# An attention pass in a graph kernel: weight and decay read from one PSUM bank, by two relus and two exponentials, in place of two banks and two exponentials

## The reference, cut to what matters

```python
f_src = (feat @ W_src.T + b_src)          # and f_dst, f_v likewise
a = f_src[src] + f_dst[dst]
e = jnp.where(a >= 0, a, 0.2 * a)         # the score of an edge
seg_max = segment_max(e, dst)
ex = jnp.exp(e - seg_max[dst])
sa = ex / segment_sum(ex, dst)[dst]
rst = segment_sum(f_v[src] * sa, dst)
```

## Time and profile before

| | |
|---|---|
| time, median of 3 runs | 4219.99 us (4213.49 to 4231.76) |
| the profiled execution | 4217.84 us, its span from first to last instruction 4216.0 us |
| busy over the span | PE 2904.7 us (69%), DVE 2103.0 us (50%), POOL 1590.1 us (38%), ACT 780.2 us (19%) |
| chain that ended last | PE 46%, DVE 18%, another core or an unknown queue 12%, DMA 11%, issue 7% |
| mean granted clock of PE | 0.780 of 2.4 GHz |

### The profile page before, as it was taken

How to read it: one execution, slowest core, us unless ns; L and a number is a source line. 1 busy time by engine, 2 the same in 40 slices (tenths; PEclk the granted TensorE clock), 3 DMA queues, 4 the chain that set the end, 5 groups by cost and what they waited for, 6 DMA issues and landing times.

```text
span 4216.0 us, 49450 instructions
## 1 busy us (share of the span) xinstructions
PE 2904.7 (69%) x14303; PEld 1742.8 (41%) x14451; DVE 2103.0 (50%) x4819; ACT 780.2 (19%) x1986; POOL 1590.1 (38%) x1665
## 2 busy tenths in 40 slices
PE   1444534444444666879677774999999999999188
PEld 1333323333333221434322222666666666666044
DVE  4555565555555322331300122777777777777420
ACT  0001101010100000100010011444444444444100
POOL 1656436666666100030000006555555556554200
PEclk6555555555555899889899956999999999999597
DMA  9940094000000899013179704778777878786142
GB/s 393 374 154 1 5 358 153 1 1 1 1 1 1 330 407 372 0 59 103 57 268 320 264 25 133 230 239 241 239 235 241 242 237 247 235 244 203 57 142 72
DMA packets 460279, 725.77 MB, mean 172 GB/s; under 512 B 64483, under 2 KB 334862, under 8 KB 460206
## 3 DMA queue, kind: packets, MB, share of 16 engines
q1 hardware_dynamic: 388154, 611.92, 41.6%
q0 software_dynamic: 65680, 109.05, 9.8%
q10 hardware_dynamic: 6372, 3.91, 0.3%
HBM read 443.75 MB, written 280.94 MB: 172 GB/s over the span
## 4 chain that ended last, share of the span: by engine, by line
PE 46%; DVE 18%; another core or an unknown queue 12%; DMA 11%; issue 7%; ACTq 2%; ACT 2%; POOL 1%; DVEq 1%; SPq 0%; POOLq 0%
DMA G<-adj_d 11%; PE PS L559 7%; DVE G L1225 6%; PE PS L738 5%; DVE G L1224 5%; PE PS L767 4%; PE PS L762 4%; PE PS L794 3%; PE PS L796 3%; PE PS L795 3%; PE PS L761 2%; PE PS L746 2%; PE PS L829 1%; PE PS L711 1%
## 5 line engine op out<-in xcount | busy, mean ns | idle before, releaser
L511 POOL DMA_INDIRECT adj_d<-D,place x782 | 748.8, 958 | 636.3 <-DVE place L1236 439.1
L498 POOL DMA_INDIRECT G<-tab_sv,src_e x784 | 748.7, 955 | 538.7 <-issue 288.4
L605 PE MATMUL PS<-wst,G 128*128 128x4 bf16 x1564 | 104.3, 171 | 637.2 <-DVE G L1225 600.2
L595 PE MATMUL PS<-ident,kst 128*128 128x128 f32 x1564 | 464.9, 453 | 86.8 <-ACT wst L1030 60.0
L595 PEld LDWEIGHTS PS<-ident,kst 128*128 128x128 f32 x1564 | 361.4, 321 | 92.8 <-ACT wst L1030 60.3
L1224 DVE SCALAR_TENSOR_TENSOR G<-PS,kst,tri 128x128 bf16<-128x128 f32 x782 | 271.0, 347 | 251.6 <-remote 146.9
L605 PEld LDWEIGHTS PS<-wst,G 128*128 128x128 bf16 x1564 | 72.3, 107 | 749.7 <-DVE G L1225 600.5
L1225 DVE TENSOR_SCALAR G<-PS,kst 128x256 bf16<-128x256 f32 x782 | 371.8, 475 | 0.0
L1440 DVE TENSOR_TENSOR_SCAN RB<-mring,RB,PS 128x512 f32<-128x512 bf16 x196 | 251.2, 1281 | 150.7 <-issue 78.9
L1029 ACT ACTIVATE kst<-G 128x2 f32 (+1 forms) x391 | 79.4, 203 | 1085.9 <-DVE place L1236 948.5
L528 POOL DMA_INDIRECT run_d<-V,head_i x25 | 24.0, 959 | 677.4 <-ACT V L1108 670.0
(11 more groups left out here) (324 smaller groups left out, 4871.9 us busy)
## 6 DMA issues: line engine op xcount, KB each, us to landing
G<-adj_d SPq DMA_DIRECT2D x350, 512.0 KB, 5.7
frac_d<-OSF SPq DMA_DIRECT2D x196, 512.0 KB
adj_d<-RB SPq DMA_DIRECT2D x7, 12800.0 KB, 54.5
run_d<-RB SPq DMA_DIRECT2D x4, 12992.0 KB
VT<-run_d SPq DMA_DIRECT2D x196, 256.0 KB
mring<-cut_d SPq DMA_DIRECT2D x196, 128.0 KB
HTx<-seg_d SPq DMA_DIRECT2D x196, 128.0 KB
OSF<-cnt_d SPq DMA_DIRECT2D x42, 512.0 KB
```

The source lines that it names most:

```text
L498: pool.indirect_dma_start(dest, None, table, bass.IndirectOffsetOnAxis(ap=idx, axis=0)).then_inc(done, 16)
L511: pool.indirect_dma_start(adj_d, bass.IndirectOffsetOnAxis(ap=place[:, w, k:k + 1], axis=0), pay[:, w, k, :], None).then_inc(sgr[g % 2], 16)
L595: last = nc.tensor.matmul(PS[:, r % 2, k * P:(k + 1) * P], kst[:, r, k:k + 1].to_broadcast([P, P]), ident[:, :], start=True, stop=True)
```

## The change

The new maximum is no longer needed for the exponentials. With d = e - (m + mring), weight = exp(-relu(-d)) and decay = exp(-relu(d)): where the score is above the old maximum, the weight is 1 and the decay exp(-d); elsewhere the decay is 1 and the weight exp(d). So PE adds only -RB(old) and -mring to bank q. ACT then reads bank q twice, relu(-d) to `D01` and relu(d) to bank 4+q, and takes the exponential of each in place. `gx` now comes after the relus, when bank q is free again; a new semaphore `gp`, after the exponentials, is what DVE's `weighted` waits for. The wait for `gback` (that `numerator` of chunk c-2 is done with bank 4+q and `D01`) goes from PE's difference matmuls; ACT has it before its first relu. `identb` becomes `nidentb`, the negative identity in bf16.

```diff
@@ PE, att_pass.body
                         if q == 0:
                             pe.wait_ge(carried, i * (R // 2) + h // 2 + 1)
-                        if not (first and h < 2):
-                            pe.wait_ge(gback, GB * (c - 2) + GB)
-                        nc.tensor.matmul(PS[:, 4 + q, :], ident[:, :], RB[:, q * CE:(q + 1) * CE], start=True, stop=False)
-                        nc.tensor.matmul(PS[:, 4 + q, :], nident[:, :], RB[:, q * CE + 1:(q + 1) * CE + 1], start=False, stop=False)
-                        nc.tensor.matmul(PS[:, q, :], nident[:, :], RB[:, q * CE + 1:(q + 1) * CE + 1], start=False, stop=True, skip_group_check=True)
-                        nc.tensor.matmul(PS[:, 4 + q, :], identb[:, :], mring[:, h, :], start=False, stop=True).then_inc(dif, 1)
+                        nc.tensor.matmul(PS[:, q, :], nident[:, :], RB[:, q * CE:(q + 1) * CE], start=False, stop=False, skip_group_check=True)
+                        nc.tensor.matmul(PS[:, q, :], nidentb[:, :], mring[:, h, :], start=False, stop=True, skip_group_check=True).then_inc(dif, 1)
@@ ACT, att_pass.body
                         act.wait_ge(dif, c + 1)
-                        nc.scalar.activation(PS[:, 4 + q, :], PS[:, 4 + q, :], ACT.Exp)
                         if not (first and h < 2):
                             act.wait_ge(gback, GB * (c - 2) + GB)
-                        nc.scalar.activation(D01[:, q, CE:2 * CE], PS[:, q, :], ACT.Exp).then_inc(gx, 1)
+                        nc.scalar.activation(D01[:, q, CE:2 * CE], PS[:, q, :], ACT.Relu, scale=-1.0)
+                        nc.scalar.activation(PS[:, 4 + q, :], PS[:, q, :], ACT.Relu).then_inc(gx, 1)
+                        act.wait_ge(gx, c + 1)
+                        nc.scalar.activation(D01[:, q, CE:2 * CE], D01[:, q, CE:2 * CE], ACT.Exp, scale=-1.0)
+                        nc.scalar.activation(PS[:, 4 + q, :], PS[:, 4 + q, :], ACT.Exp, scale=-1.0).then_inc(gp, 1)
@@ DVE, weighted
-                    dve.wait_ge(gx, c + 1)
+                    dve.wait_ge(gp, c + 1)
```

More of the change, by code:

```diff
@@ L119, in build @@
         onesb = sb("onesb", [P, TILE], bf16)
-        identb = sb("identb", [P, P], bf16)
+        nidentb = sb("nidentb", [P, P], bf16)
         nident = sb("nident", [P, P])
@@ L281, in build @@
         gx = sem("gx")
+        gp = sem("gp")
         gfront = sem("gfront")
@@ L1279, in _ @@
                 v.tensor_scalar(hdj[:, j, :], hd[:, :], float(-j * CW), None, ALU.add)
-            step(v.tensor_copy(identb[:, :], ident[:, :]))
+            step(v.tensor_copy(nidentb[:, :], nident[:, :]))
             dve.wait_ge(pst, 7)
```

## The result

| | before | after |
|---|---|---|
| median (range) | 4217.65 us (4213.49 to 4231.76) | 4363.16 us (4360.91 to 4378.95) |
| the profiled execution | 4217.84 us | 4378.95 us, span 4377.1 us |
| pace of the attention loop | 6.58 us a chunk | 7.43 us a chunk |

A forecast was written before the change was run, and what follows sets the result against it. PE at 6.30 us a chunk was taken to bound the kernel. Afterwards DMA's 5.25 + 0.28 + 0.07 of stalls make 5.60; 4217.84 - 195 x (6.58 - 5.60) = 4027, set to 4029 us for the median; range 3940 to 4135.

The forecast's parts named there:

- PE falls to 4.58 us a chunk: Attention loop: removing two f32 matmuls over 512 columns takes PE's work from 6.30 to 4.58 us a chunk.
- ACT's added 1.15 us: Attention loop: two more activations and ACT's own wait add 1.0 to 1.4 us a chunk, taken as 1.15.
- The longer chain closes at 4.85: Attention loop: the chain from maximum scan through relus and exponentials fits a 4.85 us pace, so added ACT work costs nothing.
- The DMA bound, 5.25 us: Attention loop: with PE shortened, DMA binds next, moving 1.57 MB a chunk at 299 GB/s in 5.25 us.
- The stalls, 0.35 us a chunk: Attention loop: unexplained ACT waits before `fifth` grow with ACT's list, from 0.28 to 0.35 us a chunk, added to the bound.
- the clock falls: Attention loop, chance 0.06: PE's gaps bring 1.2 GHz, 9.16 us for such a chunk; slower than before from x = 0.28.

The follow-up runs named there:

- e14: Changed kernel with POOL gathering source rows for the first four chunks only, on a slow-kind chip: 3851.35 us, ratio 0.9246.
- e8: Changed kernel with POOL gathering source rows for the first four chunks only, on a fast-kind chip: 3365.55 us, ratio 0.9223.
- e5: Changed kernel with the eight transposes of `turn_back` replaced by two f32 identity matmuls over 512 columns, on a fast-kind chip: 3476.33 us, ratio 0.9531.
- e17: Changed kernel with gathers for the first four chunks only; SP's queue loads the same 512 rows into the buffer for later chunks: 3363.63 us, ratio 0.9228.
- e2: Kernel before with two in-place copies of 512 columns added on ACT behind the exponentials, PE's list untouched: 4155.38 us, ratio 0.9991.
- e18: Changed kernel with gathers of 16 numbers a row in place of 256 behind the first four chunks, on a fast-kind chip: 3412.29 us, ratio 0.9353.
- e1: Changed kernel with two cancelling f32 matmuls over 512 columns put back, PE at 6.30 us a chunk: 4153.95 us, ratio 0.9967.
- e4: Changed kernel with two cancelling f32 matmuls over 256 columns added, PE at 5.44 us a chunk: 4309.99 us, ratio 1.0345.
- e7: Changed kernel with one zero-weight f32 matmul over 512 columns added, PE at 5.44 us a chunk, on a fast-kind chip: 3483.8 us, ratio 0.9532.
- e11: Changed kernel with one zero-weight f32 matmul over 512 columns added, PE at 5.44 us a chunk, on a slow-kind chip: 4324.7 us, ratio 1.0371.
- e13: Changed kernel, unmodified, run again against the kernel before on a slow-kind chip: 4313.95 us, ratio 1.0365.
- e3: Changed kernel without the loads of `GZ`, `mring` and `sring` behind the fourth chunk: 4287.1 us, ratio 1.0303.
- e15: Changed kernel with an extra DVE scan of 512 elements a chunk behind `numerator`, into a tile nobody reads: 4306.56 us, ratio 1.0344.

## Why the prediction was wrong, point by point

- **PE falls to 4.58 us a chunk**: right. L793 to L793 is 4.57 us in the timeline above.
- **ACT's added 1.15 us**: right. From L976 at 3011.18 to the end of L980 at 3013.42 are 2.24 us, where two exponentials took 1.08: 1.16 more. `gp` was foreseen 2.21 us behind the start of the relus.
- **The longer chain closes at 4.85**: right. e14 and e8, which have no gathers, run it at 4.82 with DVE full, and no wait for `gp` limits it.
- **The DMA bound, 5.25 us**: not tested as such. With the real gathers the shortest pace run is 5.41 (e5), where PE's own 5.44 us bind and the DMA share is 0.97. e17 moves as many bytes in 4.83 us, though in SP's loads of the same 512 rows, so the bytes alone are no bound at 5.25; 327 GB/s agrees with the dense pass of the earlier trace rows, which I had set aside.
- **The stalls, 0.35 us a chunk, "from above twice 0.28"**: this is the step that failed. I saw 66.4 us of waits that no event explains, took them for a price of ACT's instructions and let them grow with ACT's list. They are waits for PE's signals (the one of the earlier trace rows for a signal 5.26 us late). e2 has the longer list without more of them; with PE's work shortened they grew from 66.4 to 204.4 us, from 0.40 to 1.38 us a chunk, over a stretch with fewer chunks. With the slow clock behind each they make the pace 7.43 in place of 5.60. The forecast had them as a term that is added to whatever binds; the runs show that they depend on how full PE is, and so took the gain and more.
- **The rival "the clock falls"** (0.06) had the right side and half of the mechanism. Its price was 5.60 + 3.56 x with x the part of chunks at 1.2 GHz. A mean of 0.85 between the levels 1.00 and 0.50 is 0.30 of the time at 1.2 GHz. With 9.16 us for a slow chunk and 5.60 for another that is x = 0.21 of the chunks, which gives 6.3 and not 7.43. Its x was to come from PE's ordinary gaps, but e18, with PE noted busy for 557.64 of 600 us and waits of up to 2.2 us for its gathers, keeps 1.00. In the rows the clock is down behind a hold: 0.50 from 3020 to 3024 above, 0.52 from 3120 to 3127 in the kernel before. It was priced too low because the stall and the clock stood as two cases, where the one makes the other.

**What is shown and what is not.** Shown: the loss needs PE's shortened work (e1 against e4 on one chip, and against the changed kernel), a chip of the slow kind (e7 against e11, one kernel on two chips) and POOL's gathers (e14 against e13, 4.82 against 7.18 us a chunk on one chip); ACT's new list does not make it by itself (e2), and it needs neither the full DMA load (e3) nor a higher mean rate of PE instructions than before (e15). Not settled: why a full PE is nearly spared, whether the gathered bytes or POOL's instructions and descriptors hold the signals, and how much of the loss is the hold and how much the clock behind it, since no run has as many long holds at a clock of 1.00. The Trainium skill (DMA: Bandwidth & Descriptors, section "Latency and other measured facts") gives as its best guess that the descriptor rings of DMAs issued by GpSimd, which lie in SBUF, crowd the ports of two DMA engines; no run here shows that this reaches PE. The unmodified changed kernel was not run on the fast kind; e5 and e7, which keep its ACT, DVE and POOL work and have more PE time, gain 4.7% there. On the slow kind no version with its full work was faster than the kernel before by more than the 0.3% of e1.

## What to carry to other kernels

A wait that no event explains is no constant to be added: find out whose signal it is (compare the noted end of the producer with the start of every consumer) before taking away the work that hides it. Where an engine is full, shortening it can change more than its own time; price each stall together with the slow clock behind it. And where a change is worth a few per cent, run it on more than one chip: the sign was not the same on two.

## What the runs showed of the hardware that was not expected

- Two kinds of chip: the kernel before took 4158 to 4220 us on four occasions (two of them on one chip), and 3647 and 3648 us on two others, on two chips. In the kernel before, the merge passes ahead of the attention loop are what differs most: the scan starts at 2605.6 us, in e7 on the fast kind at 2101.5, in e11, the same kernel, on the slow kind at 2592.5. DVE's L1224 in those passes waits mostly for a remote signal in the changed kernel (idle time before it, 273.1 us), where e8 on the fast kind has 88.3 us, most of it put down to PE:

```profile
L1224 DVE SCALAR_TENSOR_TENSOR G<-PS,kst,tri 128x128 bf16<-128x128 f32 x782 | 270.9, 346 | 273.1 <-remote 196.2
```

  POOL's indirect DMAs run beside those passes too. From 100 to 1300 us 401 of 663 recorded signals of PE are more than 0.3 us late in the changed kernel, and none of 834 in e7 on the fast kind (the latest 0.02 us).
- On the slow kind, PE's completions reach the waiting engines 4 to 5.6 us late in the hold shown (waits of `fifth` up to 6.8 us), beside POOL's gathers; DVE's and ACT's recorded ones come within 0.01 us.
- POOL's gathers are no faster than about 1.25 us each even with a sixteenth of the bytes (e18, 5.04 us a chunk of four).
